# Where the s rows enter the attention scores: a spreading product on TensorE or a bias column on ScalarE, in a four-layer graph network on one core

## What is computed

```python
Wh = norm(x) @ W
s  = Wh @ a1                  # one number per row i
s2 = Wh @ a2                  # one number per column j
e  = s[:, :, None] + s2[:, None, :]
e  = where(adj > 0, leaky_relu(e, 0.2), very negative)
out = elu(softmax(e, axis=-1) @ Wh)
x  = x + out
```

## Time and profile before

| what | value |
|---|---|
| median of 3 runs | 587.17 us (584.67 to 588.05) |
| the profiled execution's own time | 585.35 us |
| its span, first to last instruction | 583.6 us |
| PE busy | 544.2 us (93%) |
| PE weight loads busy | 452.0 us (77%) |
| DVE busy | 447.8 us (77%) |
| ACT busy | 418.4 us (72%) |
| POOL busy | 232.1 us (40%) |
| mean granted TensorE clock, as a share of full speed | 0.985 |

### The profile page before, as it was taken

How to read it: one execution, slowest core, us unless ns; L and a number is a source line. 1 busy time by engine, 2 the same in 40 slices (tenths; PEclk the granted TensorE clock), 3 DMA queues, 4 the chain that set the end, 5 groups by cost and what they waited for, 6 DMA issues and landing times.

```text
span 583.6 us, 15065 instructions
## 1 busy us (share of the span) xinstructions
PE 544.2 (93%) x3792; PEld 452.0 (77%) x3825; DVE 447.8 (77%) x1652; ACT 418.4 (72%) x1102; POOL 232.1 (40%) x449
## 2 busy tenths in 40 slices
PE   6678999999999999999999999999977999999993
PEld 5556678777787878778777787767756799999993
DVE  3766979889898898988989888776555377777777
ACT  1355667878878788787887878877643578888883
POOL 6222214442434424334243342331322036666665
PEclk8999999999999999999999999999999799999998
DMA  8504325052250522505235051230320377777732
GB/s 202 121 14 151 95 69 165 6 160 83 82 163 1 162 79 84 159 4 162 71 91 163 0 163 35 76 110 9 102 72 2 120 223 242 247 236 218 221 119 72
DMA packets 78834, 66.46 MB, mean 114 GB/s; under 512 B 9916, under 2 KB 64460, under 8 KB 78796
## 3 DMA queue, kind: packets, MB, share of 16 engines
q1 hardware_dynamic: 65562, 60.60, 34.0%
q10 hardware_dynamic: 13234, 5.42, 3.4%
HBM read 61.57 MB, written 4.42 MB: 113 GB/s over the span
## 4 chain that ended last, share of the span: by engine, by line
PE 78%; issue 6%; DVE 5%; POOL 5%; ACT 4%; ACTq 1%; DVEq 0%; POOLq 0%
PE bank L1496 14%; PE bank L1483 13%; PE wide L206 5%; PE bank L1728 5%; PE bank L1738 4%; PE wide L1728 4%; PE wide L239 4%; PE wide L1738 4%; PE bank L1475 3%; PE bank L1476 3%; PE bank L1477 3%; PE wide L231 2%; PE wide L199 2%; PE wide L1524 2%; PE wide L220 2%
## 5 line engine op out<-in xcount | busy, mean ns | idle before, releaser
L1496 PE MATMUL bank<-w,h2w 128*128 128x128 f32 x768 | 104.2, 279 | 1.8 <-DVE h2w L1080 1.8
L1496 PEld LDWEIGHTS bank<-w,h2w 128*128 128x128 f32 x768 | 94.8, 192 | 6.9 <-DVE h2w L1080 3.0
L1483 PE MATMUL bank<-h,w 128*128 128x512 f32 x192 | 98.8, 596 | 0.3 <-ACT h L821 0.3
L816 ACT ACTIVATE h<-bank,b 128x512 f32<-128x512 f32 x96 | 66.3, 690 | 41.7 <-PE bank L1483 41.5
L821 ACT ACTIVATE h<-bank,b 128x512 f32<-128x512 f32 x96 | 66.0, 688 | 12.9 <-PE bank L1477 12.7
L1080 DVE TENSOR_TENSOR h2w<-h,wide_w 128x512 f32<-128x512 f32 x96 | 64.8, 676 | 8.2 <-ACT h L816 8.0
L1475 PE MATMUL bank<-xnTh,w1h 128*128 128x512 f32 x96 | 66.9, 697 | 0.0
L100 POOL TENSOR_TENSOR route_var_eps<-route_mean_var,eps 128x4 f32<-128x4 f32 x16 | 10.4, 651 | 115.2 <-DVE route_mean_var L93 115.1
L100 POOL TENSOR_TENSOR at_var_eps<-at_mean_var,eps 128x4 f32<-128x4 f32 x32 | 12.9, 403 | 94.0 <-DVE at_mean_var L93 94.0
L268 ACT ACTIVATE at_pr<-at_lk,at_nm 128x128 f32<-128x128 f32 x128 | 41.3, 414 | 3.6 <-DVE at_nm L303 3.6
L206 PE MATMUL wide<-at_wc,at_xT 128*128 128x130 f32 x256 | 36.0, 286 | 5.1 <-ACT at_xT L247 5.1
(11 more groups left out here) (264 smaller groups left out, 1364.0 us busy)
## 6 DMA issues: line engine op xcount, KB each, us to landing
wide_w<-w_scratch SPq DMA_DIRECT2D x96, 256.0 KB, 4.5
mask<-in_L_ffn_W SPq DMA_DIRECT2D x124, 128.0 KB, 2.4
x<-in_x SPq DMA_DIRECT2D x16, 256.0 KB, 5.1
adj_in<-in_adj SPq DMA_DIRECT2D x16, 256.0 KB, 5.8
wide_w<-bmix_scratch SPq DMA_DIRECT2D x16, 256.0 KB, 3.6
xin<-in_x SPq DMA_DIRECT2D x15, 256.0 KB, 5.6
out<-at_pr ACTq DMA_DIRECT2D x8, 256.0 KB, 3.1
out<-at_prT ACTq DMA_DIRECT2D x7, 256.0 KB, 2.8
```

What stands on the lines that cost most here:

```text
L816: a.activation(h2[:, e % 2, :], b_h2[:, :], ACT.Relu, bias=b2[:, e:e + 1]).then_inc(h2_ready, 1)
L1483: pe.matmul(b_h2[:, :], w2[:, e, :], h1[:, e % 2, :], start=True, stop=True).then_inc(l2_done, 1)
L1496: last = pe.matmul(b_out[:, s], h2w[:, e % 2, s], w3[:, e, :], start=False, stop=(e == E0 - 1), skip_group_check=True)
```

## The change

The product L220 is taken out, so that the bank holds the mask and s2 alone. ScalarE's one copy of 512 columns becomes four passes of 128 columns, one for each graph, with that graph's s column of `wh` as bias. The parts of s are still split, transposed and copied, and stand unused in `rows`; the stationary operands of the s2 products pick the others. Nothing else changes, and no instruction changes its place.

```diff
@@ attn_pe_scores @@
     pe.wait_ge(st["rows_ready"], g + 1)
     pe.matmul(st["bank"][:, :], identb[:, :], mask[:, cols(g)], start=True, stop=False, skip_group_check=True)
-    pe.matmul(st["bank"][:, :], st["rows"][:, :], spread[:, 0, :, :].rearrange("p t d -> p (t d)"), start=False,
-              stop=False, skip_group_check=True)
     for t in range(GG):
         last = pe.matmul(st["bank"][:, t * P:(t + 1) * P], spread[:, 1, t, :], st["rows"][:, :], start=False,
                          stop=True, skip_group_check=True)
@@ attn_act_z @@
     a.wait_ge(st["z_done"], g + 1)
     need(a, st["x_ready"], g)
-    a.activation(st["lk"][:, :], st["bank"][:, :], ACT.Copy).then_inc(st["z_ready"], 1)
+    for t in range(GG):
+        s = slice(t * P, (t + 1) * P)
+        last = a.activation(st["lk"][:, s], st["bank"][:, s], ACT.Identity, bias=st["wh"][:, t, P + 1:P + 2])
+    last.then_inc(st["z_ready"], 1)
```

## The result

| | before | changed |
|---|---|---|
| median, 6 runs each | 587.49 us (584.67 to 590.44) | 593.93 us (592.75 to 595.96) |
| ratio, 95% interval | | 1.0113 (1.0079 to 1.0147) |
| profiled execution, its span | 585.35, 583.6 us | 592.75, 591.0 us |

The change costs 1.1%, 6.4 us by the medians and 7.4 us between the two profiled executions; forecast were +9.1, a time of 596, and a range from 587 to 602. Of the 7.4, the edit can't account for all: the first copy of the rows, ahead of every changed instruction, starts at 14.73 in the changed kernel's profile and at 15.49 in the other.

The account below looks back on a forecast made before the run. ACT's queue, hidden behind PE's 99%, was taken to set the pace: 12 (c - 0.12) + 12 (c - 0.37) + 2c + 2 (c - 0.21) = +9.1 us, giving 596 us by the median, range 587 to 602.

Parts of the forecast that it names:

- the two waits that were named: PE's loads for transposing the probabilities (waiting for ACT's exponentials) and for `layer2` (waiting for `relu1`), forecast to start later.
- place A: Second attention's scores (at1), copied in a gapless ACT queue ahead of the exponentials; forecast 0.43 us later each time.
- c: Extra ACT time per place, four bias passes less one copy; forecast 0.55 us, range 0.16 to 0.69.
- place B: First attention's scores (at0), copied on ACT just ahead of `relu1`, which `layer2` needs; forecast 0.18 us later each time.
- c - 0.12: PE's delay at place A in each of 12 rounds, via exponentials and a dry array; 0.43 us.
- c - 0.37: PE's delay at place B in each of 12 rounds, via `relu1` and `layer2`; 0.18 us.
- The count of places: How often each delay counts: 12 at place A, 12 at place B, two at 2c, two at c - 0.21; sum +9.1 us.
- c - 0.21: Very first and very last round, where ACT waits for the scores: ACT's extra time less the product's 0.21 us.
- 2c + (c - 0.21): Last three rounds: two where PE already waits for exponentials and all of c counts, then the very last.
- Never better than -0.21: Floor at place B: removing the product can gain PE at most its own 0.21 us there.
- the rivals: Cheap passes (585 to 587 us, chance 0.11), PE alone bounding (584, 0.05), dear Identity (611, 0.05), PE's clock falling (no chance).
- The faster rival: PE's 99% is what it seems, ACT's idle time absorbs the passes: -3.2 us, 584 by the median; chance 0.05.

Follow-up runs that it names:

- e1: Kernel before with the change in the second attention only (place A), the first keeping product and copy; 24.94 us a round, ratio 1.0107.
- e2: Kernel before with the change in the first attention only (place B), the second keeping product and copy; 24.71 us a round, ratio 1.0079.
- e8: Changed kernel with ACT's pooling alone moved behind the exponentials of place A; 24.73 us a round, ratio 1.0087 against before.
- e4: Kernel before, product kept, its one copy replaced by four passes with a bias column of zeros; 25.12 us a round, ratio 1.0137.
- e5: Changed kernel with four plain Copy passes, no bias column, s left out of the scores; 24.41 us a round, ratio 1.0004 against before.
- e11: e3 with DVE's weighing of the fourth expert moved ahead of the ranking of the routing logits; 24.21 us a round, ratio 0.9914 against before.
- e3: Kernel before with the product L220 removed and nothing in its place, one copy kept; 24.37 us a round, ratio 0.9979.
- e6: Changed kernel, ACT reordered: pooling behind place A's exponentials, third expert's first-layer relu ahead of place B's scores; 24.41 us a round, ratio 1.0038 against before.
- e10: e7 with DVE's weighing of the fourth expert moved ahead of the ranking of the routing logits; 24.40 us a round, ratio 0.9978 against before.
- e9: e6 with DVE's weighing of the fourth expert moved ahead of the ranking of the routing logits; 24.38 us a round, ratio 1.0015 against before.
- e7: Kernel before with the same two ACT steps moved as in e6, nothing else; 24.53 us a round, ratio 1.0005.
- e12: e9 with product and one copy kept in the filling and draining rounds; 24.37 us a round, ratio 0.9995 against before.

## Why the prediction was right

- **The bound.** That PE's 99% hid an ACT queue without slack was right: e1 and e2 find the cost behind the two waits that were named, e8 takes away the loss at place A by making room in front of the exponentials, and e4 shows the product free beside the passes.
- **The price c.** 0.55 was forecast from the last layer's passes, 0.53 measured. The passes average 0.368 us, but ACT's busy time rose by 18 us (436.6 against 418.4), not the 28 I named, because time in which two passes overlap is counted once in it (the 128 passes of 0.368 are listed with 36.3 us). The Trainium skill's 93 ns for a pointer operand ("ScalarE: Activation LUTs", section "What ACT_TABLE_LOAD costs") agrees with the 0.10 between e5's passes and the changed kernel's. The estimate of 0.29 for a pass from that section's figures is above the 0.25 measured here, so the trace was the better guide to the sum.
- **Place A and place B.** c - 0.12 = 0.43 and c - 0.37 = 0.18 were forecast, 0.44 and 0.18 measured. The match to the hundredth is in part luck: with the measured c of 0.53 the same formulas give 0.41 and 0.16. The period of 25.1 came as 25.15. The dry start of PE's array at place A, taken from one late round, is 0.66 in all ten rounds. PE's share in the rounds fell to 247.44 of 251.53, 98.4%, where some 97% was forecast. And e11, where DVE is out of the way and c is nothing, has -0.12 to -0.14 at place A, which is what c - 0.12 gives for it.
- **The count of places.** This is the term that was mis-sized. The sum had 9.1 for the 7.4 between the two profiles, and the starts of the copy of the rows show where the 1.7 went. At the first copy the changed kernel's execution is 0.76 ahead, and no changed instruction has run yet. From there to the ten rounds it loses 1.24 where 1.56 was forecast (c - 0.21, two places A and two places B). In the ten rounds it is 6.18 for 6.1. Behind them, up to the routing of the last layer, it is 1.07 for the 2c + (c - 0.21), some 1.4, of the sum. The last layer, in which nothing was changed, is 0.3 shorter. So 0.6 of the 1.7 is the sum's mistake at the ends, and 1.1 lies where the edit does nothing. Part of the mistake is in the first two full rounds: place A gave 0.00 and 0.33 there, place B -0.23 and +0.05. In the first of them no group is pooled yet and ACT's queue at place A is not closed (0.37 idle for PE in the kernel before); I counted its place A in full.
- **A part that was wrong without showing.** "Never better than -0.21" was the floor at place B, and -0.12 that of place A with c at nothing. Place B's held to 0.02 (-0.23 at most, in e3). Place A's did not, in e3 and e6: DVE's weighing ended 0.05 ahead of PE's load, and by e10 it already held that load back by 0.14. What was wrong is that place A was priced with ACT alone behind it, and DVE left out. It had no weight with c at 0.53, since ACT was later still, but the rivals rested on it. The faster rival's 584 could not have come by this kernel, and my expectations for e3, e6, e8, e9 and e10 failed on it.

## What to carry to other kernels

An engine at 99% sets the pace only if none of the loads that it issues starts a few hundredths of a microsecond behind another engine's result; look at those starts, since here such a hold of 0.14 us was not listed as a wait. Work that moves from such an engine to another one is priced by where it lands in the other's queue: the same four passes cost 0.43 us ahead of the exponentials and 0.18 ahead of a ReLU, while the other engine was idle for a fifth of the time. And before work is taken off the bound engine, take it out alone, with nothing in its place: here that was worth 0.17 of a possible 0.42 us a round, and with the work in this order no replacement did better.

## What the runs showed that I had not expected

The clock of TensorE in the filling of the pipeline. The steps of a full round repeat between e7 and the kernel before to 0.02 us, but the ten rounds start up to 3 us later than before (129.77 before, 132.78 in e8), and e7, where the order alone differs, 1.4 later. By the starts of the copy of the rows, e8 loses 2.3 us against before between the second and the third copy, e1 and e5 1.7 and 1.6 between the third and the fourth. The rows of these stretches (first before, then e8, then e1) have the granted clock as the seventh figure:

```profile
32.00:48.00 16.00, 11.45 (x67) 7.66 (x66) 12.07 (x44) 9.64 (x22) 4.26 (x8) 1.00 0.30 94
48.00:72.00 24.00, 21.93 (x131) 16.69 (x133) 18.51 (x67) 14.45 (x28) 5.58 (x10) 1.00 0.27 82
```

```profile
32.00:48.00 16.00, 13.44 (x65) 9.31 (x63) 9.68 (x34) 8.75 (x23) 1.95 (x4) 0.79 0.13 39
```

```profile
48.00:72.00 24.00, 22.76 (x127) 17.25 (x129) 17.03 (x63) 13.75 (x27) 5.01 (x9) 0.93 0.20 60
```

A mean of 0.79 over 16 us is some 6.7 us at the lower of the two levels (1.2 and 2.4 GHz), 0.93 over 24 us some 3.4, and the time lost is a third to a half of that. Where the clock stayed at 1.00 in both stretches (before, changed, e3, e4, e12) no such step appears in them; e4 has one of 1.0 between the first and the second copy, which I cannot place. It comes and goes between kernels whose filling differs little, e10 and e12 for instance (0.93 and 1.00 in the second stretch), so in a single profile 1 to 3 us outside the full rounds say nothing about an edit. e2's profile has such a step too (1.67 us, clock 0.93) and a clock of 0.77 between 440 and 464 us (0.86 in the kernel before), where it loses another 1.3. e1 and e9 lose 1.2 and 1.3 there, at 0.80 and 0.72. Whether an edit makes the dips more frequent, which e2's and e9's medians would suggest, the runs leave open: each kernel has one trace, and the clock of an execution's filling is seen only there.
